# Neighbour maximum by table look-up: tables of 64 subsets against tables of 32

## The reference, cut to what matters

```python
m1z = z @ W1.T + b1
m2z = z @ W2.T + b2
pair = relu(m1z[:, :, None, :] + m2z[:, None, :, :])
mask = (swapaxes(P, 1, 2) != 0)[..., None]
m = max(where(mask, pair, -inf), axis=2)
return relu(concatenate((z, m), axis=-1) @ Wu.T + bu)
```

## Time and profile before

| | before |
|---|---|
| median of 3 runs | 2234.93 us |
| the profiled execution | 2239.13 us |
| its span | 2237.3 us |
| PE matmul busy | 1857.5 us (83%) |
| VectorE (DVE) busy | 1892.8 us (85%) |
| ScalarE (ACT) busy | 1568.4 us (70%) |
| granted TensorE clock, mean | 0.936 |

### The profile page before, as it was taken

How to read it: one execution, slowest core, us unless ns; L and a number is a source line. 1 busy time by engine, 2 the same in 40 slices (tenths; PEclk the granted TensorE clock), 3 DMA queues, 4 the chain that set the end, 5 groups by cost and what they waited for, 6 DMA issues and landing times. The chain is left out here.

```text
span 2237.3 us, 43782 instructions
## 1 busy us (share of the span) xinstructions
PE 1857.5 (83%) x13411; PEld 1155.8 (52%) x13419; DVE 1892.8 (85%) x2726; ACT 1568.4 (70%) x3389; POOL 334.0 (15%) x282
## 2 busy tenths in 40 slices
PE   2978888888867888886799999999999577877886
PEld 2857777777754555665544444444444233333346
DVE  5978888888876999997899999999999466666766
ACT  0634554455436888883499999999999577777773
POOL 1510000000001110103322222222221000000001
PEclk9979999999986999996699999999999799999998
DMA  6000000000000000000155555555555799999982
GB/s 170 0 8 1 1 0 0 0 0 0 0 1 13 6 4 5 5 5 19 49 209 204 216 202 211 206 212 204 212 206 206 268 358 349 345 353 348 353 288 78
DMA packets 122539, 297.25 MB, mean 133 GB/s; under 512 B 20352, under 2 KB 56456, under 8 KB 122264
## 3 DMA queue, kind: packets, MB, share of 16 engines
q1 hardware_dynamic: 105336, 287.69, 34.3%
q10 hardware_dynamic: 16896, 8.39, 1.3%
q0 software_dynamic: 256, 0.56, 0.1%
HBM read 154.78 MB, written 141.82 MB: 133 GB/s over the span
## 5 line engine op out<-in xcount | busy, mean ns | idle before, releaser
L1239 DVE TENSOR_TENSOR v_pairs<-hd 128x2048 f32 (+1 forms) x128 | 291.8, 2280 | 0.0
L1244 DVE TENSOR_TENSOR v_pairs<-hd 128x2048 f32 (+1 forms) x128 | 291.4, 2277 | 0.0
L1300 ACT ACTIVATE v_hid<-v_psW 128x1024 f32<-128x1024 f32 x256 | 265.5, 1037 | 18.1 <-PE v_psW L1341 9.6
L724 DVE TENSOR_REDUCE m_part<-m_psS 128x128 f32<-128x1024 f32 (+1 forms) x192 | 216.9, 1130 | 67.1 <-PE m_psS L603 67.0
L1341 PE MATMUL v_psW<-v_pairs,p_w1T 128*64 128x512 f32 x1024 | 247.5, 600 | 26.8 <-DVE v_pairs L1239 26.8
L1303 ACT ACTIVATE v_junk<-v_psW 128x1024 bf16<-128x1024 f32 x256 | 266.4, 1041 | 0.0
L603 PE MATMUL m_psS<-m_onehot,m_tableT 64*128 64x128 f32 x2816 | 217.3, 293 | 34.2 <-DVE m_part L724 18.0
L1341 PE MATMUL v_psW<-v_pairs,l_w1T 128*64 128x512 f32 (+1 forms) x1024 | 243.2, 587 | 0.0
L956 ACT ACTIVATE a_ex<-a_eu,a_nmx 128x128 f32<-128x128 f32 x512 | 197.8, 390 | 42.2 <-PE a_psA L925 34.3
L1224 POOL COPY v_weights<-p_split 128x192 bf16 (+1 forms) x64 | 154.0, 2407 | 476.9 <-PE v_psW L1341 466.6
L1483 DVE SCALAR_TENSOR_TENSOR s_hid<-s_hid 128x1024 f32<-128x1024 f32 x128 | 155.8, 1221 | 66.6 <-ACT s_hid L1543 66.6
(11 more groups left out here) (251 smaller groups left out, 3573.9 us busy)
## 6 DMA issues: line engine op xcount, KB each, us to landing
pair_hidden<-v_hid SPq DMA_DIRECT2D x256, 512.0 KB, 2.6
s_h<-pair_hidden SPq DMA_DIRECT2D x128, 1024.0 KB, 7.4
s_wide<-pair_scores SPq DMA_DIRECT2D x64, 128.0 KB, 6.0
adj_ring<-in_adj_dram ACTq DMA_DIRECT2D x16, 256.0 KB, 5.0
x_all<-in_x_dram ACTq DMA_DIRECT2D x16, 256.0 KB, 5.3
out_dram<-o_res SPq DMA_DIRECT2D x16, 256.0 KB, 2.3
pair_scores<-s_rot SPq DMA_DIRECT2D x64, 32.0 KB, 6.0
p_ends<-in_c_ends_dram SPq DMA_DIRECT2D x1, 1024.0 KB, 4.7
```

The lines of the kernel that those rows point to most:

```text
L724: nc.vector.tensor_reduce(part[:, i, r, :], psS[:, 2 * (at % 2):2 * (at % 2) + 2, 0:w].rearrange("z q (c i) -> z i q c", i=N), AX.XY, ALU. ...
L1239: nc.vector.tensor_tensor(slab(s), one, far, ALU.max).then_inc(max_done, 1)
L1244: nc.vector.tensor_tensor(slab(s), one, far, ALU.subtract).then_inc(sub_done, 1)
L1300: nc.scalar.activation(hid[:, s, :], psW[:, buf, :], ACT.Identity, accum_out=hsum[:, bass.ds(m, 1)]).then_inc(evacuated, 1)
```

## The change

Blocks have 5 nodes and tables 32 entries; block k holds the nodes k, k+28, k+56, k+84 and k+112 (strided, so m2 needs no padding; the fifth exists for 16 of the 28 blocks). Four blocks make a chunk: 7 chunks a graph, in two items of 4 and 3, and 8 items a quad. A chunk is selected by four products over 32 rows, each into its own bank of psS; all four banks belong to one item, and select waits for the reduce of the item just before. The merge of two items is one tensor_tensor. The bias is put into psU by a product of a row of ones with `bu`, and DVE adds relu(psU) to x directly. The pieces of the neighbouring quads are spread anew.

```diff
-BLK = 6
-NBLK = (N + BLK - 1) // BLK
+BLK = 5
+NBLK = 28
-NCH = NBLK // 2
+NCH = NBLK // 4
...
-        blk, t = divmod(j, BLK)
+        t, blk = divmod(j, NBLK)
...
+        one = sb("one", [1, N])
+        both = sb("both", [C, QC])
...
                 def select(g, i, r):
-                    pe.wait_ge(reduced, done(n - 2))
-                    for c in range(4 * r, min(4 * r + 4, NCH)):
-                        for q in (0, 1):
+                    pe.wait_ge(reduced, done(n - 1))
+                    for c in chunks(r):
+                        for q in range(4):
                             rows = slice(SUB * q, SUB * q + SUB)
-                            last = nc.tensor.matmul(psS[:, 2 * par + q, b(c % 4)], tableT[rows, par, c % 4, :],
+                            last = nc.tensor.matmul(psS[:, q, b(c % 4)], tableT[rows, par, c % 4, :],
                                                     onehot[rows, par, c % 4, :], start=True, stop=True)
...
                 def update(g, p):
+                    pe.wait_ge(added, done(g - 1))
+                    nc.tensor.matmul(psU[:, :].rearrange("n (b c) -> n b c", c=C), one[:, :],
+                                     k.bu[0:1, :].unsqueeze(1).broadcast_to([1, G, C]), start=True, stop=False)
                     pe.wait_ge(mT_ready, done(g))
-                    pe.wait_ge(biased, done(g - 1))
...
 PE quad:
-                        if at == NG - 1 and prev:
-                            update(g - 1, 1 - p)
-                        if at == NG - 1 and next:
-                            turn(g + 1, 1 - p)
-                        if at == NG and next:
+                        if at == 0 and next:
+                            turn(g + 1, 1 - p)
+                        if at == 1 and prev:
+                            update(g - 1, 1 - p)
+                        if at == 2 and next:
                             second(g + 1, 1 - p)
-                        if at == NG + 1 and next:
+                        if at == 3 and next:
                             first(g + 1, 1 - p)
...
 DVE:
-                        nc.vector.tensor_tensor(table[:, i, 0:NBLK, w:2 * w], table[:, i, 0:NBLK, 0:w],
-                                                node[:, :, t:t + 1].broadcast_to([C, NBLK, w]),
+                        nc.vector.tensor_tensor(table[:, i, 0:blocks, w:2 * w], table[:, i, 0:blocks, 0:w],
+                                                node.broadcast_to([C, blocks, w]),
...
-                    nc.vector.tensor_reduce(mx[:, b(i)], part[:, i, :, :].rearrange("z r i -> z i r"), AX.X,
-                                            ALU.max).then_inc(merged, 1)
+                    nc.vector.tensor_tensor(mx[:, b(i)], part[:, i % 2, 0, :], part[:, i % 2, 1, :], ALU.max).then_inc(merged, 1)
...
-                    nc.vector.tensor_tensor(
-                        upd[:, :].rearrange("n (b c) -> n b c", c=C), psU[:, :].rearrange("n (b c) -> n b c", c=C),
-                        k.bu[:, :].unsqueeze(1).broadcast_to([N, G, C]), ALU.add).then_inc(biased, 1)
...
 DVE quad, after reduce(g, at), for the 8 items:
+  at 0: add_own(g-1), tables(g, 2, LATE)        at 1: merge 0, tables(g, 3, EARLY)
+  at 2: tables(g, 3, LATE)                      at 3: merge 1, tables(g+1, 0, EARLY)
+  at 4: update(g-1), tables(g+1, 0, LATE)       at 5: merge 2, tables(g+1, 1, EARLY), statistics(g-1)
+  at 6: tables(g+1, 1, LATE)                    at 7: merge 3, tables(g+1, 2, EARLY)
```

More of the change, by code:

```diff
@@ L525, in phase_maxpass @@
             "grown", "tabled", "t_turned", "tT_ready", "match_mm", "onehot_ready"))
-        selected, reduced, merged, summed, mT_ready, u_mm, biased, added = (sem(n) for n in (
-            "selected", "reduced", "merged", "summed", "mT_ready", "u_mm", "biased", "added"))
+        selected, reduced, merged, summed, mT_ready, u_mm, added = (sem(n) for n in (
+            "selected", "reduced", "merged", "summed", "mT_ready", "u_mm", "added"))
         b = lambda i: slice(i * N, (i + 1) * N)
         ITEMS = G * NG
+        chunks = lambda r: range(4 * r, min(4 * r + 4, NCH))
         def quads(eng, quad):
@@ L650, in second @@
                     act.wait_ge(tabled, done(g * G - (G + 1)))
-                    act.wait_ge(padded, 1)
-                    nc.scalar.activation(m2[:, p, :, 0:N], psF[:, :].rearrange("z (b n) -> z b n", n=N), ACT.Identity,
-                                         bias=k.b2[:, 0:1]).then_inc(m2_copied, 1)
+                    nc.scalar.activation(m2[:, p, :], psF[:, :], ACT.Identity, bias=k.b2[:, 0:1]).then_inc(m2_copied, 1)
                 def first(g, p):
@@ L672, in update @@
                     act.wait_ge(u_mm, done(g - 2))
-                    nc.scalar.activation(mT[:, p, :], mx[:, :], ACT.Relu).then_inc(mT_ready, 1)
+                    nc.scalar.activation(mT[:, p, :], both[:, :], ACT.Relu).then_inc(mT_ready, 1)
                 def quad(g, p, prev, next):
@@ L679, in quad @@
                             update(g - 1, 1 - p)
-                        if at == NG and next:
+                        if at == 2 and next:
                             relu(g + 1, 1 - p)
-                        if at == NG + 1 and next:
+                        if at == 3 and next:
                             second(g + 1, 1 - p)
-                        if at == NG + 2 and next:
+                        if at == 4 and next:
                             first(g + 1, 1 - p)
@@ L693, in _ @@
             def _(dve):
-                for s in (tabled, reduced, merged, summed, biased, added):
+                for s in (tabled, reduced, merged, summed, added):
                     dve.sem_inc(s, BIAS)
+                nc.vector.memset(one[:, :], 1.0)
                 nc.vector.memset(table[:].rearrange("z b k s -> z (b k s)"), 0.0).then_inc(padded, 1)
                 dve.wait_ge(padded, 1)
-                nc.vector.memset(table[:, :, 0:NBLK, 0], LOWEST)
-                nc.vector.memset(m2[:, :, :, N:PADN].rearrange("z p b j -> z (p b) j"), LOWEST).then_inc(padded, 1)
+                nc.vector.memset(table[:, :, 0:NBLK, 0], LOWEST).then_inc(padded, 1)
                 dve.wait_ge(padded, 2)
@@ L736, in add_own @@
+                    nc.vector.tensor_tensor(mx[:, b(i)], part[:, i % 2, 0, :], part[:, i % 2, 1, :], ALU.max).then_inc(merged, 1)
                 def add_own(g, p):
                     dve.wait_ge(merged, done(g * G + (G - 1)))
-                    nc.vector.tensor_tensor(mx[:, :], mx[:, :], m1[:, p, :], ALU.add).then_inc(summed, 1)
+                    dve.wait_ge(mT_ready, done(g - 1))
+                    nc.vector.tensor_tensor(both[:, :], mx[:, :], m1[:, p, :], ALU.add).then_inc(summed, 1)
@@ L768, in quad @@
                                 add_own(g - 1, 1 - p)
-                            tables(g, p, G - 1, EARLY)
+                            tables(g, p, 2, LATE)
                         if at == 1:
[L771 to L779, removed]
+                            merge(g, 0)
+                            tables(g, p, 3, EARLY)
+                        if at == 2:
+                            tables(g, p, 3, LATE)
+                        if at == 3:
+                            merge(g, 1)
+                            if next:
+                                tables(g + 1, 1 - p, 0, EARLY)
+                        if at == 4:
+                            if prev:
+                                update(g - 1)
+                            if next:
+                                tables(g + 1, 1 - p, 0, LATE)
+                        if at == 5:
+                            merge(g, 2)
+                            if next:
+                                tables(g + 1, 1 - p, 1, EARLY)
+                            if prev:
+                                statistics(g - 1)
+                        if at == 6 and next:
+                            tables(g + 1, 1 - p, 1, LATE)
+                        if at == 7:
+                            merge(g, 3)
+                            if next:
+                                tables(g + 1, 1 - p, 2, EARLY)
+                for i in range(2):
                     tables(0, 0, i)
+                tables(0, 0, 2, EARLY)
                 quads(dve, quad)
```

46 lines of the change are left out of this document (18 added, 28 removed).

## The result

The changed kernel takes 2227.34 us (median of 8 runs, 2222.59 to 2236.19) against 2234.99 us (8 runs, 2232.69 to 2239.95): ratio 0.9965, 95% interval 0.9949 to 0.9982, 7.7 us less. The forecast was 21 us less (2214). The sign was right and the range held the time, but the gain is about a third of the forecast.

The account below looks back on a forecast made before the run. DVE was taken to set the pace, with PE making it wait. A quad of 28.5 us at full clock plus 1.3 for clock falls gave 29.8 against 31.1, 21 us less over 16 quads: 2214 us, range 2188 to 2262.

Parts of the forecast that it names:

- DVE's work: DVE's reduces, tables, merges and other passes per quad: 26.1 us, a win of 5.0 a quad were DVE never to wait.
- Four at once: PE's selections: four products over 32 rows overlap, so 32 records take 1.19 us and 24 take 0.97.
- The two rivals built on slower or fewer overlaps: PE's selections: steps of four at 0.145 us, 2233 us, chance 0.12; or only two at once, 2272 us, chance 0.12.
- the rival of two at once: PE's selections overlap only two products: 2.09 or 1.64 us each, 33.4 us a quad, 2272 us; chance 0.12.
- Gaps and update chain: DVE between reduces: gaps of 11.0 us a quad, plus a stall of about 0.9 from PE's update ahead of select(2).
- The hand-over from a reduce to its selection: Between DVE and PE: 0.05 us each way, making gaps at least 1.29 us before long items, 1.07 before short.
- DVE's wait for selections: Sign in the profile after: 2.0 us a quad, some 32 us at full clock, nearer 55 with the falls.
- The clock: PE half busy in items 4 to 6: clock falls in two quads of three, back before the update's products; 1.3 us a quad.
- The rival in which the clock stays low through the update: Clock returns only behind PE's update: 3.9 us a quad on top of 28.5, giving 32.4 and 2256 us; chance 0.14.
- The gaps at 0.50: Slow gaps 5, 6, 7 and 0 between reduces cost 0.2 + 0.7 + 0.9 + 0.2 = 2.0 us.
- the factor 2/3: Share of quads expected to have a clock fall, turning 2.0 us a fall into 1.3 us a quad.
- the 31.1: Time per quad of the layer before the change, from 498 us for 16 quads; the forecast set 29.8 against it.

Follow-up runs that it names:

- e2: The changed kernel with GpSimd's normalization started behind selection 2 instead of in item 0: 2225.46 us, ratio 0.9953 to the kernel before.
- e6: The changed kernel with PE's update cut in two, GpSimd's normalization started later, and idle products in items 0, 4, 6, 7: 2175.83 us, ratio 0.9739.
- e10: e6 without its later GpSimd start, so the normalization begins in item 0 again: 2186.36 us, ratio 0.9769 to the kernel before.
- e8: The changed kernel with idle PE products in items 0 and 4 to 7, and GpSimd's normalization started behind selection 2: 2196.21 us, ratio 0.9832.
- e7: The kernel before, with select waiting for the reduce of the item just before, as with one set of banks: 2248.83 us, ratio 1.0061.
- e9: The kernel before with idle PE products in items 0, 1, 9, 10, 11: 2215.04 us, ratio 0.9894 to the kernel before.
- e1: The changed kernel with idle PE products that nothing reads after selections 4 to 7 of each quad: 2205.04 us, ratio 0.9859.
- e5: The changed kernel with PE's update cut in two: bias and hT products in own items 5 and 6, mT products left in next quad's item 1: 2208.32 us.
- e3: The changed kernel with selection products ordered two row groups at a time instead of four: 2332.91 us, ratio 1.0423 to the kernel before.

## Why the prediction was wrong in size

- **DVE's work: right.** Every piece within 0.02 us of its forecast, but for the statistics (13.1 us over 14 quads, 0.94 each where 0.86 was forecast) and the table step that GpSimd disturbs, which was not foreseen. In this kernel it is hidden (e2); in a better one it costs 7 to 12 us (e6, e10).
- **Four at once: right.** 1.17 and 0.95 us for 32 and 24 records, as forecast (1.19, 0.97). The Trainium skill, TensorE: Matmul & The Clock Gate, Measured speedup vs the span model, has 3.07 times for four products of 512 columns. Here, with 128 columns, 32 records over 32 rows took 1.17 us where 16 over 64 rows took 1.16, so no such loss is seen, and the measurement decides. The two rivals built on slower or fewer overlaps are out. (In the rival of two at once the terms add up to 33.6 us a quad, not 33.4.)
- **Gaps and update chain: right in sum, in part by luck.** Items 0 and 1 together have gaps of 3.9 us both in the kernel after and in e8; forecast 1.55 + 2.19 = 3.7. At full clock the quad was forecast at 28.5 and is 28.3 (e8). Two errors cancel in it. The hand-over from a reduce to its selection took 0.15 us, not the 0.05 read from one place, so gaps 2, 3, 6 and 7 were 1.15, 1.47, 1.15 and 1.46 in e8 where 1.07 and 1.29 by turns were forecast. And DVE's pieces overlap by some 0.1 us each in the timeline, so gaps 4 and 5 were 1.27 and 1.77 instead of 1.55 and 1.93. The sign for it was DVE's wait for selections: 56.2 us in e8 where 32 were forecast for full clock. The single set of banks costs the kernel before, with its twelve items, 1.8 us a quad (e7 against e9); in the forecast this cost stands inside the gaps.
- **The clock: the term that failed.** "I expect a fall there in two quads of three ... 2.0 x 2/3 = 1.3 us a quad." It fell in every quad, in the place given, came back in item 0 as expected, and cost 2.3 (e8). The reason given was the thin PE work of items 4 to 6; e1 and e8 bear it out, where filling items 4 to 7 kept the clock up in them. The rival in which the clock stays low through the update came true in the last quad alone (low from 602.94 to 623.42 us, gap 1 of 5.35 us). The gaps at 0.50 were priced well behind items 6 and 7 and too low behind item 5 (0.2 + 0.7 + 0.9 us forecast; kernel after less e8: 0.6 + 0.7 + 0.9). The size was wrong, not the mechanism: 1.0 us a quad, 16 us in all, of which the factor 2/3 is 0.7 a quad and the price of a fall (2.3 instead of 2.0) the rest.
- **The sum against the layer.** From the first reduce to the end of the last, the forecast is 16 x 29.8 = 477 us and the kernel after took 489.3 (498.8 before). Of these 12.5 us too much, the fourteen whole quads from the second on brought 11.1 (30.6 each instead of 29.8: the clock 1.0 more, the rest 0.2 less), the first quad took 1.0 less, and the last 2.4 more.
- **The last quad.** The sum took 16 equal quads. The last has no piece of a next one on PE, and its clock was 0.67 in the profile after: 30.4 us from its first reduce to its last, against 24.8 before. By the gaps of full clock (e8), some 6 us of the 30.4 are the clock's; this is an estimate. But the clock is not the only cost of such a quad: in e7, with one set of banks and a clock of 1.00, the last quad of the kernel before took 28.2 us instead of 24.8: DVE has no tables of a next quad to do while it waits, and the gaps behind items 5 to 10 were 1.1 to 1.4 us where they had been 0 to 0.9. With the tail, the last quad took 6.8 us more than before; the 15 others gained 15.9 together (473.0 to 457.1), the start 0.4: 9.6 in all.
- **A match that is luck.** Quad for quad, the middle of the layer went from 31.9 us to 30.6, and 1.3 is what the forecast said. But it had 29.8 against 31.1: the 31.1 is 498 us over 16 and so mixes the short first and last quads in, and the 29.8 lacks 0.8 us. The clock stood in the kernel before too: 1.5 us of the 31.9 are lost to its falls (e9), and the measured 498 us hold them.

## What to carry to other kernels

When two engines hand one buffer back and forth and the change thins out the matmul work, reckon the case in which the stretch with the least PE work is slow in every round, not only in some; here it was. Price the gaps there from rows at the lower clock. Real PE work that has slack (products whose operands are ready early) can fill that stretch (e5, 20 us) as well as idle products can (e1, 24 us); remember the last round, which has no next one to fill it. A collision or a wait that costs nothing today can be on the path once its cover is removed, as the GpSimd start was (e2 alone nothing, e6 against e10 7 to 12 us): try such edits together too, not only one by one. And a sum that comes out right is not a proof of its terms; check them one by one in the profile after.

## What the runs showed of the hardware

- Products over 32 rows in four row groups ran four at a time in 4-byte floats: 32 records in 1.17 us, where 16 records over 64 rows took 1.16. With the queue ordered two groups at a time the same 32 records took 1.72 us.
- In e3 the clock stayed at 0.50 (1.2 GHz) over 23.90 us with PE busy 20.93 of them, and it stayed there behind a stretch busy 3.41 of 3.41 us, while before it came back behind 3.42 of 3.42. Busy time in the profile alone does not tell when it returns; which property of the work does was not tried.
- In the kernel after the falls came every 30.72 us and the mid-layer quads every 30.5 to 30.7 (30.6 in the mean), where before the quads ranged from 30.4 to 33.2. The fall moved slowly, from 18.1 us behind the first reduce of the second quad to 19.8 behind that of the fifteenth; whether one rhythm draws the other along was not tried.
- GpSimd's and DVE's two-operand passes in SBUF slow each other (from 1.04 to between 1.41 and 1.50 us, and from 0.84 to 1.69 us for two table steps); beside a reduce out of PSUM GpSimd's first pass kept its 1.04 us. The one that began second was the one stretched: add_own began 0.17 us ahead of GpSimd's pass and kept its 0.68 us, and where in e10 the pass began 0.14 us ahead (at 241.82 us), it kept 1.04 and add_own took 1.44.
